# Unit rows in 32 buffers instead of 16, half of each activation cast on ScalarE, landings reported two units late

## The reference

```
x = x + gnn(_layernorm(x), adj, ...)          # two 128x128 products per graph, gates, relu
xf = _layernorm(x).reshape(-1, 128)           # 16384 tokens of 128 numbers
gate_logits = xf @ Wg + bg
top_w, top_i = jax.lax.top_k(gate_logits, 2)
top_w = jax.nn.softmax(top_w, axis=-1)
for e in range(8):
    h = gelu(xf @ W1[e] + b1[e], exact)       # 128 -> 512
    out = out + w_dense[:, e:e + 1] * (h @ W2[e] + b2[e])
x = x + out
```

## Time and profile before

| | |
|---|---|
| median of 3 runs | 718.91 us (718.31 to 721.46) |
| the profiled execution | 719.69 us, of which the span from first to last instruction is 717.8 |
| busy share of the span | PE 91%, DVE 85%, ACT 75%, POOL 70% |
| mean granted TensorE clock | 0.962 |
| chain that ended last, by engine | PE 32%, ACT 23%, POOL 13%, issue 12%, DMA 10%, DVE 8% |

### The profile page before, as it was taken

The page is one execution under the profiler, slowest core; times in us unless marked ns, Lnnn a source line. Parts: engine busy times, 40 slices in busy tenths (PEclk is TensorE's granted clock), DMA queues, the critical chain, the costliest instruction groups (busy, mean ns, idle before and its releaser), DMA issues.

```text
span 717.8 us, 17809 instructions
## 1 busy us (share of the span) xinstructions
PE 654.3 (91%) x4879; PEld 596.8 (83%) x4879; DVE 608.5 (85%) x2041; ACT 541.3 (75%) x1505; POOL 504.2 (70%) x471
## 2 busy tenths in 40 slices
PE   5979898988859999899997999988999999999991
PEld 4646566666539999899997999988999999999991
DVE  5899999999986888987885888885888888888881
ACT  4689999999977978788674767664777776767670
POOL 2553777676764577778887888877777777777774
PEclk9999999999977999999998999998999999999997
DMA  8999995558346897959999975789764444444211
GB/s 293 336 357 279 354 345 180 178 177 309 107 148 182 288 327 254 310 163 300 325 353 319 370 240 159 219 320 354 241 160 128 122 129 120 125 128 125 72 42 33
DMA packets 85497, 161.06 MB, mean 224 GB/s; under 512 B 32631, under 2 KB 36736, under 8 KB 85392
## 3 DMA queue, kind: packets, MB, share of 16 engines
q1 hardware_dynamic: 66032, 112.96, 50.2%
q0 software_dynamic: 18496, 46.70, 17.8%
q10 hardware_dynamic: 864, 0.21, 0.1%
HBM read 104.95 MB, written 57.23 MB: 226 GB/s over the span
## 4 chain that ended last, share of the span: by engine, by line
PE 32%; ACT 23%; POOL 13%; issue 12%; DMA 10%; DVE 8%; SPq 1%; POOLq 0%; DVEq 0%; ACTq 0%
POOL out_dram L688 8%; ACT hs L750 6%; POOL rows L691 5%; ACT row L759 5%; ACT t_loop L741 4%; PE bank L1623 4%; PE bank L1624 4%; PE bank L1625 4%; PE bank L1637 4%; PE bank L1638 4%; PE bank L1642 4%; ACT t_in L734 3%; DMA rows<-row,to_row 3%; PE bank L1609 2%; PE bank L1653 2%
## 5 line engine op out<-in xcount | busy, mean ns | idle before, releaser
L846 ACT ACTIVATE act_f<-bank,b_t 128x256 f32<-128x256 f32 x560 | 220.1, 476 | 22.8 <-PE bank L1625 14.7
L688 POOL DMA_INDIRECT out_dram<-row,to_row x140 | 165.7, 1184 | 57.7 <-issue 56.1
L646 POOL DMA_INDIRECT rows<-row,slot_low x128 | 136.8, 1069 | 62.6 <-issue 34.4
L1429 DVE TENSOR_TENSOR act_lo<-act_f,act_hi 128x1024 fp32r<-128x1024 f32 x140 | 171.9, 1228 | 5.9 <-ACT act_hi L852 0.2
L1422 DVE CAST act_hi<-act_f 128x1024 fp32r<-128x1024 f32 (+1 forms) x140 | 90.5, 647 | 70.1 <-ACT act_f L846 67.7
L836 ACT ACTIVATE in_hi<-bank 128x256 fp32r<-128x256 f32 x140 | 53.9, 385 | 113.4 <-PE bank L1609 113.1
L1623 PE MATMUL bank<-in_hi,w_t 128*128 128x256 f32 x376 | 115.6, 308 | 7.5 <-DMA w_t<-w_split 7.5
L691 POOL DMA_INDIRECT rows<-row,to_row x76 | 94.6, 1245 | 24.7 <-issue 20.9
L1624 PE MATMUL bank<-in_lo,w_t 128*128 128x256 f32 x376 | 107.4, 286 | 0.0
L1625 PE MATMUL bank<-in_hi,w_t 128*128 128x256 f32 x376 | 107.4, 286 | 0.0
L1637 PE MATMUL bank<-act_hi,w_t 128*128 128x256 f32 x376 | 100.9, 302 | 0.1
(11 more groups left out here) (278 smaller groups left out, 1762.2 us busy)
## 6 DMA issues: line engine op xcount, KB each, us to landing
row<-rows SPq DMA_DIRECT2D x108, 260.0 KB, 3.0
w_t<-w_split SPq DMA_DIRECT2D x52, 512.0 KB, 6.3
w_up<-w_split SPq DMA_DIRECT2D x28, 512.0 KB, 6.1
xs<-in_x_dram SPq DMA_DIRECT2D x16, 512.0 KB, 4.7
x_t<-in_x_turned_dram SPq DMA_DIRECT2D x16, 512.0 KB, 6.3
rows<-ends_rep SPq DMA_DIRECT2D x15, 260.0 KB, 7.7
xs<-rows SPq DMA_DIRECT2D x10, 260.0 KB
b_t<-in_biases_dram SPq DMA_DIRECT2D x140, 2.5 KB
```

Source lines behind the costliest of these rows:

```text
L646: pool.indirect_dma_start(out=rows, out_offset=bass.IndirectOffsetOnAxis(ap=slot_low[:, r, b:b + 1], axis=0), in_=row[:, r, b, :], in_offs ...
L688: pool.indirect_dma_start(out=out_rows, out_offset=at, in_=got[:, g, j, P:2 * P], in_offset=None, bounds_check=TOKENS - 1, oob_is_err=Fals ...
L846: last = act.activation(act_f[:, s, c, :], ps_h(t, half)[:, i, :], ACT.Gelu, bias=b_t[:, w, c:c + 1])
L1429: dve.tensor_tensor(act_lo[:, s], act_f[:, t.slot(2)], act_hi[:, s].bitcast(F32), ALU.subtract).then_inc(s_hlo, 1)
```

## The change

Four edits. Rows of units from 32 on go round 32 places (`lane`): units 32 to 47 in `got` as before, 48 to 63 in `first_rows`, 64 to 79 in `got`, and so on; so the load of unit k waits for unit k-32, from unit 48 on. ACT casts the first half of the activations in every unit and VectorE the second, so both waits (`s_half`) hold in all units. POOL reports, and waits for, the landing of the unit two before instead of three before. `EARLY` goes from 12 to 24.

```diff
-    EARLY = 3 * GR // 4
+    EARLY = 24
...
+    LANES = 2 * GR
...
+    def lane(k):
+
+        return k % GR if k < NE else (GR + k - NE) % LANES
+
+    def uses(k):
+
+        return sum(lane(i) == lane(k) for i in range(k))
...
         def rows_of_unit(t):
-            return first_rows[t.slot(GR)] if t.index < NE else got[:, t.slot(GR)]
-        to_row = sb("to_row", [P, GR, BLK], I32)
+            i = lane(t.index)
+            return first_rows[i] if i < GR else got[:, i - GR]
+        to_row = sb("to_row", [P, LANES, BLK], I32)
...
-                    if not NE <= t.index < NE + GR:
-                        wait_slot(sp, s_out, 16 * BLK, t, 0)
+                    if uses(t.index):
+                        sp.wait_ge(s_out[lane(t.index)], 16 * BLK * uses(t.index))
...
             def landed(t):
-                wait_slot(pool, s_out, 16 * BLK, t, 16 * BLK)
+                pool.wait_ge(s_out[lane(t.index)], 16 * BLK * (uses(t.index) + 1))
                 pool.sem_inc(s_landed, 1)
 
             def scatter(t):
                 second = t.index >= NU
-                if 0 <= t.index - 3 < NU:
-                    landed(t.back(3))
+                if 0 <= t.index - 2 < NU:
+                    landed(t.back(2))
                 wait_turn(pool, s_done, 1, t, 1)
-                g = t.slot(GR)
+                g = lane(t.index)
...
-                if t.index < NE:
-
-                    wait_turn(act, s_act, 2, t, 1)
-                    wait_turn(act, s_mm2, 1, t, -LATE)
-                    act.activation(act_hi[:, t.slot(LATE + 1), 0:FC // 2], act_f[:, s, 0:FC // 2], ACT.Copy).then_inc(s_half, 1)
+                wait_turn(act, s_act, 2, t, 1)
+                wait_turn(act, s_mm2, 1, t, -LATE)
+                act.activation(act_hi[:, t.slot(LATE + 1), 0:FC // 2], act_f[:, s, 0:FC // 2], ACT.Copy).then_inc(s_half, 1)
...
-                done = FC // 2 if t.index < NE else 0
+                done = FC // 2
                 dve.tensor_copy(act_hi[:, t.slot(LATE + 1), done:], act_f[:, t.slot(2), done:]).then_inc(s_hhi, 1)
```

More of the change, by code:

```diff
@@ L263, in program @@
         got = row[:, 1:5].rearrange("p r (s j) k -> p (r s) j k", j=BLK)
-        got_i = got.bitcast(I32)
         first_rows = []
@@ L400, in program @@
         s_done = sem("unit_summed")
-        s_out = [sem(f"unit_rows_scattered{i}") for i in range(GR)]
+        s_out = [sem(f"unit_rows_scattered{i}") for i in range(LANES)]
         s_landed = sem("first_pass_units_landed")
@@ L600, in _ @@
                         rows_in(unit(k + AHEAD), early[k + AHEAD - NU] if 0 <= k + AHEAD - NU < AHEAD else now[i])
-            for i in range(GR):
-                sp.wait_ge(s_out[i], 16 * BLK * ((UNITS + GR - 1 - i) // GR))
+            for k in range(UNITS - LANES, UNITS):
+                sp.wait_ge(s_out[lane(k)], 16 * BLK * (uses(k) + 1))
         @block.gpsimd
@@ L687, in scatter @@
                     if second:
-                        pool.indirect_dma_start(out=out_rows, out_offset=at, in_=got[:, g, j, P:2 * P], in_offset=None,
+                        pool.indirect_dma_start(out=out_rows, out_offset=at, in_=rows_of_unit(t)[:, j, P:2 * P], in_offset=None,
                                                 bounds_check=TOKENS - 1, oob_is_err=False).then_inc(s_out[g], 16)
@@ L1426, in hidden_lo @@
                 wait_turn(dve, s_hhi, 1, t, 1)
-                if t.index < NE:
-                    wait_turn(dve, s_half, 1, t, 1)
+                wait_turn(dve, s_half, 1, t, 1)
                 dve.tensor_tensor(act_lo[:, s], act_f[:, t.slot(2)], act_hi[:, s].bitcast(F32), ALU.subtract).then_inc(s_hlo, 1)
             def sum_up(t):
-                g, second = t.slot(GR), int(t.index >= NU)
+                g, second = lane(t.index), int(t.index >= NU)
                 held = rows_of_unit(t)
@@ L1437, in sum_up @@
                     i = t.index if second else t.index - NE
-                    dve.scalar_tensor_tensor(out=to_row[:, g, :], in0=skip[:, i, :], scalar=BIG, in1=got_i[:, g, :, at],
+                    dve.scalar_tensor_tensor(out=to_row[:, g, :], in0=skip[:, i, :], scalar=BIG, in1=held.bitcast(I32)[:, :, at],
                                              op0=ALU.mult, op1=ALU.max)
@@ L1631, in layer2 @@
                 wait_turn(pe, s_hhi, 1, t, 1)
-                if t.index < NE:
-                    wait_turn(pe, s_half, 1, t, 1)
+                wait_turn(pe, s_half, 1, t, 1)
                 wait_turn(pe, s_y, 1, t, 0)
```

## The result

The change takes 745.01 us (median of four runs, 743.09 to 745.91) against 719.54 for the kernel before on the same chip; the ratio is 1.0341, 95% interval 1.0311 to 1.0371. The profiled execution took 743.09, its span is 741.3, against 719.69 and 717.8. TensorE's share falls to 88%, GpSimd's to 67%: both wait more.

A forecast was written before the change was run, and what follows sets the result against it. The second pass was taken to wait for unit 66's landing, so POOL's pace up to it sets the time. Terms 2.3 + 3.7 + 11.7 + 3.9 - 4.4 = +17.2 on 719.69 gave 737 us, range 721 to 750.

The forecast's parts named there:

- What bounds the kernel: Second pass starts when unit 66's scatter has landed; everything after it is a fixed length of full PE.
- the sum: Terms for POOL up to unit 66's landing: 2.3 + 3.7 + 11.7 + 3.9 - 4.4 = +17.2 us.
- 32 places: SP's gap before unit 48's load goes, worth 0 to PE; POOL loses the stall's relief, +2.3 us.
- The lead: PE, without its first stall, 6.7 us ahead: unit 74 at 475.3 instead of 483.8, still waiting for unit 66.
- ACT's cast and EARLY at 0: 108 more casts of 0.65 hide in ACT's idle 0.90 before in_hi; EARLY costs at most one table read.
- Landings two units late: POOL's scatters wait for the landing two units before: +3.7, +11.7 and +3.9 us, then -4.4 made up.
- from there to 433 I take half of the time: After 380 us, landings slow half the time until 433: 78.5 us slow in all from 328, +11.7 us.
- two units take L + 2.15: POOL's pace when waiting: L from second scatter to landing, 0.88 to restart, 1.27 to the next second scatter.
- landings quicken: Rival, chance 0.12: fewer scatters in flight land sooner; at L of 4.2 the wait costs only +2 to +4.
- Units 8 to 13: Units 8, 9, 12 and 13, between first-stage scatters, need 3.48 instead of 2.54 us: +3.7 us.
- POOL speeds up: Rival, chance 0.07: VectorE's cast holds POOL up, so the shorter cast makes it faster, 713 us, at most 705.
- The 2.98: Landing time seen with queues nearly empty; the lower bound for L, at which only 2.3 stays, 722 us.

The follow-up runs named there:

- three-late run: The whole change, but with landings reported three units late as in the kernel before: 719.26 us, ratio 1.0006 to the kernel before.
- The last experiment: The whole change (landings two units late) with act_lo made by two instructions of half the width: 735.5 us, ratio 1.0223 to the kernel before.

## Why the prediction was right, point by point

*What bounds the kernel.* Right. Unit 66's landing sets the start of the second pass: it moved by 21.6 us, and what follows it only by 1.9. Undoing the one edit that moves it gives all of the time back. Of the 23.5 us the sum had 17.2, nearly three quarters.

*32 places.* Right that they remove the first gap on SP and that TensorE gains next to nothing by it; the run of the places alone shows that. The lead itself didn't come about, which no step foresaw: the scatter of unit 14, behind the first stage's, is later, unit 30's row load waits 11.3 for it in the first fence of waits, and TensorE, which waits behind that load on SP's queue, loses 6.7 us before unit 27 (a step of 9.99 instead of 3.26). So unit 74 came at 483.42, not at 475.3, and SP's gap began at 472.79 and not near 463. It costs nothing, for the same reason for which the lead is worth nothing. Neither the 0.024 us per unit of the second pass nor the 1.0 at the end was in the sum.

*ACT's cast and EARLY at 0.* The cast is covered as forecast (0.41 left before `in_hi`); alone it even gives 2 us. `EARLY` at 24 is part of the three-late run, which shows no price beyond those of the cast and the places; alone it wasn't run.

*Landings two units late.* The mechanism is right: each bound unit starts 0.88 after the landing of the unit two before it, at 33 of units 6 to 66. The terms were too small: by 2.4 up to unit 14 and by 2.8 from there to unit 58; 0.8 more than forecast was then made up before unit 66's landing, and 1.9 came behind it. Unit 60 was 26.3 us later (484.51 against 458.23), not 10 to 20.

The step that was mis-sized is the length of the slow stretch, "from there to 433 I take half of the time". All of it was slow. Busy time in the change by window, the last two columns being the DMA engines' busy share and GB/s:

```profile
328.00:380.00 52.00, 51.97 (x441) 51.55 (x440) 40.51 (x89) 44.73 (x112) 30.17 (x27) 1.00 0.96 328
380.00:435.00 55.00, 54.93 (x470) 54.69 (x469) 43.82 (x102) 47.33 (x118) 32.94 (x30) 1.00 0.92 314
435.00:462.00 27.00, 27.00 (x232) 27.00 (x231) 20.95 (x49) 23.44 (x60) 21.40 (x18) 1.00 0.45 138
462.00:479.00 17.00, 16.72 (x143) 16.48 (x142) 12.88 (x30) 14.31 (x37) 8.92 (x9) 1.00 1.00 355
```

In these four stretches (units 18 to 31, 31 to 46, 46 to 54 and 54 to 58) a unit took 3.91, 3.74, 3.29 and 4.18: the wait cost time where the DMA engines were at 0.92 or more, and next to nothing where they were at 0.45. The forecast had 3.83 for the first and half of the second, no cost for the third, 4.2 for the fourth. With all 105 us from 328 to 433 its own rule gives 15.6 instead of 11.7. The trace of the kernel before already had a share of 0.98 from 393 to 421, as high as the 0.96 from 328 to 380:

```profile
393.00:421.00 28.00, 28.00 (x243) 28.00 (x243) 24.39 (x50) 19.61 (x52) 22.68 (x18) 1.00 0.98 343
```

That the pace itself came out, 3.82 from unit 18 to unit 46 where 3.83 was forecast, is luck in part. Landings were a little sooner than assumed, 5.2 on the mean of units 18 to 45 instead of 5.5; between 328 and 380 us, first scatters included, to set beside the earlier trace rows:

```profile
DMA to landing us min/median/max: 3.9/5.7/6.6
```

And "two units take L + 2.15" counts both scatters at 0.97. In units 15 to 44 of the change a second scatter landed 3.98 after its end, so the formula gives (3.98 + 0.88 + 0.97 + 0.30 + 0.97) / 2 = 3.55; with the 1.10 and 1.13 that the scatters took on the mean it gives 3.70, and 3.76 was measured. A POOL that waits for landings is still held up by `act_lo`, against what the rival "landings quicken" assumed. The last experiment shows it from the other side: shorter holds shorten the waiting units too.

*Units 8 to 13.* 6.1 us instead of 3.7, or 7.7 counted from unit 0's `act_lo`, which is 1.6 earlier in that execution. POOL waits for landings twice among them, 2.6 and 1.7 us beyond the usual 0.30 (at 272.71 and 297.59 in POOL's rows), in all 4.3 against the 3.7; the rest is scatters, some of the first stage, that `act_lo` held up.

*The rivals.* "Landings quicken": they did, by 0.6 us of 3.9, where 1.3 of 5.5 were needed. The 2.98 that spoke for it was not seen with queues "nearly empty": from 314 to 318 us the DMA engines' share was 0.45. "POOL speeds up": the place was right and the instruction wrong. It is `act_lo`, and the cast at most by the 2 us of its own run, that holds POOL up, and with `act_lo` halved unit 78's load goes out 12.6 us earlier than in the earlier trace rows and the time falls by 1.4%. The Trainium skill's page "SBUF — State Buffer", under "Who interferes with whom", says that a VectorE instruction with two SBUF inputs contends with a GpSimd instruction that reads SBUF; the rows of `act_lo` agree, 1.67 beside one long instruction and 1.15 beside two short ones.

## What to carry to other kernels

A wait for an engine's own transfer costs nothing on a queue in order as long as (landing + restart + issue) / distance stays under the pace of the bound, here 3.26 us: at three units back it did, at two it took 3.68 on the mean of units 14 to 58, at one 5.94, and the time went from 719 to 745 and 905. At two the cost lay where the DMA engines were full, so look at their share along the whole stretch before its length goes into a sum. Put into that sum the issue times as the trace shows them, held-up ones too. A stall that stands ahead of a later wait is worth nothing unless that wait ends sooner, and a long instruction beside an engine it holds up may be cheaper in two pieces. The Trainium skill's page "DMA: Bandwidth & Descriptors", under "Rules for kernel authors", advises to issue a DMA early and wait on its semaphore late; these three distances agree.

## What the runs showed of the hardware that was not expected

A scatter of POOL that starts inside an `act_lo` ends 0.84 us after that instruction does; with two `act_lo` of 0.689 us it ends 0.84 after the first, and VectorE pays only 0.15 us a unit for the second instruction. Six scatters of the change that start within 0.04 us of the start of an `act_lo` take 0.97 and end before it does. A tile made twice as wide, though half of it is not touched, lengthened the steps of TensorE's full stretch from 3.256 to 3.273 us in its one run; the cause stays open. With 32 places, and their 16 semaphores more, the end behind the last scatter took 8.15 us instead of 7.17; which of them costs it stays open.
